# A two-layer gated attention block: the second phase's second MLP product in bf16, split by GpSimd

## What is computed

```python
x = x + tanh(g_ffn[0])   * L0_ffn(layernorm(x))           # fp8 rounding, 256 -> 256
x = x + tanh(g_xattn[1]) * L1_xattn(layernorm(x), ctx)    # q from x, k and v from ctx
h = layernorm(layernorm(x))
y = silu(h @ w1 + fc1_bias)                               # 256 -> 1024
z = y @ w2 + fc2_bias                                     # 1024 -> 256, the second product
x = x + tanh(g_ffn[1]) * (h_residual + 0.5 * z)
```

## Time and profile before

| | us |
|---|---|
| median of 3 runs | 1995.82 (1994.78 to 1996.55) |
| the profiled execution | 1995.66 |
| its span, first to last instruction | 1993.9 |
| TensorE busy | 1727.0 (87%) |
| VectorE busy | 1318.9 (66%) |
| ScalarE busy | 1058.8 (53%) |
| GpSimd busy | 635.6 (32%) |

### The profile page before, as it was taken

One profiled execution on the slowest core, in us unless ns is written; L12 is line 12 of the kernel. 1 busy time (PEld: TensorE's weight loads), 2 busy tenths in 40 slices (PEclk: granted clock), 3 DMA queues, 4 the chain that ended last, 5 costly groups with the idle time before them and its releaser, 6 DMA issues.

```text
span 1993.9 us, 41731 instructions
## 1 busy us (share of the span) xinstructions
PE 1727.0 (87%) x14464; PEld 1336.9 (67%) x14464; DVE 1318.9 (66%) x3182; ACT 1058.8 (53%) x1886; POOL 635.6 (32%) x1236
## 2 busy tenths in 40 slices
PE   3899999999999613679989989899899998998987
PEld 2788888888888512346667666666676666766756
DVE  4677777777777463676676766667767676676532
ACT  3666666666666401445455455554554555545553
POOL 3465665656564312212212122122121221221100
PEclk9999999999999855889999999999999999999999
DMA  5212222121210022433233342342333423323200
GB/s 166 80 54 79 61 71 69 62 77 55 79 46 2 22 97 53 74 65 70 59 74 61 68 73 59 63 68 58 74 59 72 68 58 64 68 58 75 54 12 17
DMA packets 183700, 126.87 MB, mean 64 GB/s; under 512 B 14918, under 2 KB 182860, under 8 KB 183372
## 3 DMA queue, kind: packets, MB, share of 16 engines
q1 hardware_dynamic: 183628, 125.91, 27.3%
HBM read 100.68 MB, written 25.17 MB: 63 GB/s over the span
## 4 chain that ended last, share of the span: by engine, by line
PE 47%; DVE 7%; issue 4%; ACT 2%; SPq 1%; DMA 1%; POOL 1%; DVEq 0%; ACTq 0%; POOLq 0%
PE b_bank L1361 15%; PE b_bank L1441 11%; PE b_bank L1430 6%; DVE b_nm L1263 4%; PE b_scoreT L1408 3%; PE b_bank L1369 3%; PE b_score L1391 2%; PE b_scoreT L1412 2%; ACT b_E L1140 2%; PE b_bank L1520 1%; PE b_bank L1496 1%; DVE b_on L1307 1%; DVE b_st L1221 1%; PE b_bank L1471 1%; DMA b_K<-k_dram 1%
## 5 line engine op out<-in xcount | busy, mean ns | idle before, releaser
L1263 DVE TENSOR_REDUCE b_nm<-b_score 128x4 bf16<-128x1024 f32 x256 | 314.2, 1227 | 147.1 <-PE b_score L1391 147.1
L1140 ACT ACTIVATE b_E<-b_scoreT 128x1024 f32<-128x1024 f32 x256 | 262.0, 1023 | 240.5 <-PE b_scoreT L1412 239.2
L1441 PE MATMUL b_bank<-f,b_Y 128*128 128x256 f32 x1024 | 243.1, 381 | 1.0 <-ACT b_Y L1199 1.0
L31 ACT ACT_TABLE_LOAD x156 | 200.1, 1283 | 63.4 <-PEq L787 50.9
L700 PE MATMUL bank<-W2T,G 128*128 128x256 f32 x1024 | 231.4, 379 | 0.0
L1071 POOL TENSOR_TENSOR b_pool_fence<-b_pool_fence 128x1 f32<-128x1 f32 x96 | 18.8, 195 | 622.3 <-DVE b_mv L1226 622.3
L700 PEld LDWEIGHTS bank<-W2T,G 128*128 128x128 f32 x1024 | 192.0, 190 | 24.9
L1441 PEld LDWEIGHTS b_bank<-f,b_Y 128*128 128x128 f32 x1024 | 185.1, 190 | 23.3 <-ACT b_Y L1199 1.3
L667 PE MATMUL bank<-hT,W1T 128*128 128x256 bf16 x1536 | 178.3, 273 | 7.9 <-DVE hT L593 3.4
L1361 PE MATMUL b_bank<-b_hT,f 128*128 128x256 bf16 x1536 | 175.4, 275 | 2.9 <-DVE b_hT L1286 1.5
L667 PEld LDWEIGHTS bank<-hT,W1T 128*128 128x128 bf16 x1536 | 147.7, 98 | 36.6 <-ACT G L511 15.7
(11 more groups left out here) (215 smaller groups left out, 3452.4 us busy)
## 6 DMA issues: line engine op xcount, KB each, us to landing
b_Q<-q_dram SPq DMA_DIRECT2D x256, 64.0 KB, 3.4
b_K<-k_dram SPq DMA_DIRECT2D x256, 64.0 KB, 3.6
xin<-in_x SPq DMA_DIRECT2D x32, 256.0 KB, 4.8
X<-in_x SPq DMA_DIRECT2D x32, 256.0 KB, 4.6
ctxn<-in_ctx SPq DMA_DIRECT2D x32, 256.0 KB, 2.8
mask_in<-in_mask SPq DMA_DIRECT2D x32, 256.0 KB, 3.1
ctxt<-in_ctxT SPq DMA_DIRECT2D x32, 256.0 KB, 4.5
b_ctxt<-in_ctxT SPq DMA_DIRECT2D x32, 256.0 KB, 2.8
```

The source lines that it names most:

```text
L31: act.add_instruction(mybir.InstLoadActFuncSet(name=nc.get_next_instruction_name(), act_func_set_id=which, ins=[], outs=[]))
L1140: nc.scalar.activation(E[:, pair:pair + 2], scoreT_ps[:, :, :, :], ACT.Exp).then_inc(sig["E"], 1)
L1263: nc.vector.tensor_reduce(pair, score_ps[:, :, :, :], AX.X, ALU.max, negate=True).then_inc(sig["nm"], 1)
L1441: nc.tensor.matmul(bank6[:, t], Y[:, k, tile(t)], f2[:, k], start=k == 0, stop=False)
```

## The change

The second product is made of three bf16 terms. f2 becomes two bf16 halves, high and low, made in the setup by two more VectorE steps. A new tensor YT holds Y's halves. GpSimd makes them in four groups `split(b, j)`, each for two of the eight chunks of Y: a fence, a copy to bf16, a difference. Splits 0 and 1 of a batch stand at the end of its h iteration, behind cT and ahead of the group that ends in b_rh; splits 2 and 3 at the very start of the next one. `product` then makes for each chunk the terms high x high, high x low, low x high: 48 matmuls of 128x128 by 128x256 in bf16 in place of 16 in float32.

The four pieces of the product move from slots 0 to 3 to slots 4, 5, 7 and 8. In exchange the k projection moves from slot 5 to slot 1, with its copy and difference (ScalarE slot 1, VectorE slot 2), and cT is made one iteration earlier, behind b_y. b_res moves from slot 4 to slot 9 of VectorE, the transposes of b_on go to bank 7, and SyncE stores k's spill ahead of q's and the output behind the 16 loads.

```diff
-    f2 = sb("f2", [P, HC, D], F32)
+    f2 = sb("f2", [P, 2, HC, D], BF16)
...
-            step(V_.tensor_tensor(f2[:, :, :], w_2[:, :, :], sc_2[:, :, :], ALU.mult))
+            step(V_.tensor_tensor(w_2[:, :, :], w_2[:, :, :], sc_2[:, :, :], ALU.mult))
+            step(V_.tensor_copy(f2[:, 0], w_2[:, :, :]))
+            step(V_.tensor_tensor(f2[:, 1], w_2[:, :, :], f2[:, 0], ALU.subtract))
...
-            6: [("res", L_OUT, 1, 1), ("klo", L_QKV, 1, 1), ("onlo", L_PROJ, 1, 1), ("Y", L_MLP, 4, 1),
-                ("Y", L_MLP, 4, 4)],
+            6: [("klo", L_QKV, 1, 1), ("res", L_OUT, 1, 1), ("Y", L_MLP, 4, 1), ("Y", L_MLP, 4, 4)],
             7: [("yT", L_FFN, 1, 1), ("ob", L_FFN, 1, 1), ("qlo", L_QKV, 1, 1), ("on", L_PROJ, 2, 2),
-                ("nmT", L_MAX, 1, 1), ("Y", L_MLP, 4, 2)],
+                ("onlo", L_PROJ, 1, 1), ("nmT", L_MAX, 1, 1), ("Y", L_MLP, 4, 2)],
...
@@ GpSimd @@
-                if q:
-                    pool.wait_ge(sig[f"ctxt{q.parity}"], landed(q))
...
+                def split(b, j):
+                    pool.wait_ge(sig["Y"], done(b, per=HC // 2, part=j + 1))
+                    if j == 0:
+                        if (due := done(b, back=1)) is not None:
+                            pool.wait_ge(sig["f2_mm"], due)
                     fence()
+                    nc.gpsimd.tensor_scalar(YT[:, 0, 2 * j:2 * j + 2], Y[:, 2 * j:2 * j + 2], 1.0, 0.0,
+                                            ALU.mult, ALU.add).then_inc(sig["Yhi"], 1)
+                    pool.wait_ge(sig["Yhi"], done(b, per=HC // 2, part=j + 1))
+                    nc.gpsimd.tensor_tensor(YT[:, 1, 2 * j:2 * j + 2], Y[:, 2 * j:2 * j + 2], YT[:, 0, 2 * j:2 * j + 2],
+                                            ALU.subtract).then_inc(sig["Ylo"], 1)
+                if w:
+                    split(w, 2)
+                    split(w, 3)
                 if f:
...
+                if f:
+                    pool.wait_ge(sig[f"ctxt{f.parity}"], landed(f))
...
+                if h:
+                    split(h, 0)
+                    split(h, 1)
                 if o:
                     pool.wait_ge(sig["mv3"], done(o))
...
@@ ScalarE @@
-                        if j == 0:
-                            if (due := done(h, back=1)) is not None:
-                                act.wait_ge(sig["f2_mm"], due)
+                        if (due := done(h, back=1, per=HC // 2, part=j + 1)) is not None:
+                            act.wait_ge(sig["Ylo"], due)
...
@@ TensorE @@
                 def second_product(t, piece):
                     if t == 0 and piece == 0:
-                        free(6, 0)
-                        pe.wait_ge(sig["Y"], done(w, per=HC // 2))
+                        free(6, 1)
+                    if t == 0:
+                        pe.wait_ge(sig["Ylo"], done(w, per=HC // 2, part=2 * piece + 2))
                     half_ = range(HC // 2 * piece, HC // 2 * (piece + 1))
-                    for k in half_:
-                        nc.tensor.matmul(bank6[:, t], Y[:, k, tile(t)], f2[:, k], start=k == 0, stop=False)
+                    product(bank6[:, t], lambda s, k: YT[:, s, k, tile(t)], lambda s, k: f2[:, s, k], half_,
+                            start=piece == 0, stop=False)
...
+                    if slot == 1 and q:
+                        free(6, 0)
+                        pe.wait_ge(sig["ctlo"], done(q))
+                        projection(bank6, 1, 1, cT, "k_mm")
...
-                    if slot < 4 and w:
-                        second_product(slot // 2, slot % 2)
+                    if w:
+                        for i, at in enumerate((4, 5, 7, 8)):
+                            if slot == at:
+                                second_product(i // 2, i % 2)
```

More of the change, by code:

```diff
@@ L1034, in iteration @@
                         sig[f"mask{q.parity}"], 16)
+                    sp.wait_ge(sig["klo"], done(q))
+                    sp.dma_start(k_dram[q.parity].rearrange("s (c p) n -> p (s c) n", p=P),
+                                 ks[:, :, :, :].rearrange("p s c n -> p (s c) n")).then_inc(sig[f"spill{q.parity}"], 16)
                     sp.wait_ge(sig["qlo"], done(q))
@@ L1060, in iteration @@
                                 sig[f"stack{q.parity}"], 16)
+                if w:
+                    sp.wait_ge(sig["res"], done(w))
+                    sp.dma_start(out_d[bass.ds(w.number, 1)].rearrange("o p t d -> p (o t) d"),
+                                 res[:, :, :]).then_inc(sig[f"out{w.parity}"], 16)
             pipeline(sp, iteration, NB, LAGS)
@@ L1150, in iteration @@
                         nc.scalar.activation(xT[:, 0], bank8[:, :, :], ACT.Copy).then_inc(sig["xhi"], 1)
+                    if slot == 1 and q:
+                        act.wait_ge(sig["k_mm"], done(q))
+                        if (due := landed(q, back=1, per=2)) is not None:
+                            act.wait_ge(sig[f"spill{1 - q.parity}"], due)
+                        nc.scalar.activation(ks[:, 0], bank6[:, :, :], ACT.Copy).then_inc(sig["khi"], 1)
                     if slot == 3 and h:
@@ L1160, in iteration @@
                         nc.scalar.activation(qs[:, 0], bank7[:, :, :], ACT.Copy).then_inc(sig["qhi"], 1)
-                    if slot == 5 and q:
-                        act.wait_ge(sig["k_mm"], done(q))
-                        nc.scalar.activation(ks[:, 0], bank6[:, :, :], ACT.Copy).then_inc(sig["khi"], 1)
                     if slot == 10 and o:
@@ L1264, in iteration @@
                                                     negate=True).then_inc(sig["nm"], 1)
+                    if slot == 2 and q:
+                        dve.wait_ge(sig["khi"], done(q))
+                        nc.vector.tensor_tensor(ks[:, 1], bank6[:, :, :], ks[:, 0], ALU.subtract).then_inc(sig["klo"], 1)
                     if slot == 3 and f:
@@ L1292, in iteration @@
                         nc.vector.tensor_tensor(qs[:, 1], bank7[:, :, :], qs[:, 0], ALU.subtract).then_inc(sig["qlo"], 1)
-                    if slot == 6 and q:
-                        dve.wait_ge(sig["khi"], done(q))
-                        nc.vector.tensor_tensor(ks[:, 1], bank6[:, :, :], ks[:, 0], ALU.subtract).then_inc(sig["klo"], 1)
+                    if slot == 9 and w:
+                        dve.wait_ge(sig["f2_mm"], done(w))
+                        dve.wait_ge(sig["base"], done(w))
+                        if (due := landed(w, back=1)) is not None:
+                            dve.wait_ge(sig[f"out{1 - w.parity}"], due)
+                        nc.vector.scalar_tensor_tensor(res[:, :, :], bank6[:, :, :], half_gate[:, 0:1], Xb(w),
+                                                       ALU.mult, ALU.add).then_inc(sig["res"], 1)
                     if slot == 8 and o:
@@ L1311, in iteration @@
                         dve.wait_ge(sig["onhi"], done(o))
[L1312 removed]
+                        nc.vector.tensor_tensor(oT[:, 1], bank7[:, :, :], oT[:, 0], ALU.subtract).then_inc(sig["onlo"], 1)
                 if n:
@@ L1447, in hidden @@
                 def hidden(j):
-                    free(*((6, 3), (7, 5), (8, 3), (6, 4))[j])
+                    free(*((6, 2), (7, 6), (8, 3), (6, 3))[j])
                     if j == 0:
@@ L1508, in iteration @@
                         projection(bank7, 0, 0, xT, "q_mm")
-                    if slot == 5 and q:
-                        free(6, 1)
-                        pe.wait_ge(sig["ctlo"], done(q))
-                        projection(bank6, 1, 1, cT, "k_mm")
                     if slot in (6, 7) and o:
@@ L1522, in iteration @@
                     if slot == 10 and o:
-                        free(6, 2)
+                        free(7, 4)
                         pe.wait_ge(sig["on"], done(o, per=T))
-                        transposed(bank6, on, "onT_mm")
+                        transposed(bank7, on, "onT_mm")
                     if slot == 12 and m:
-                        free(7, 4)
+                        free(7, 5)
                         pe.wait_ge(sig["nm"], done(m, per=NP))
```

30 lines of the change are left out of this document (9 added, 21 removed).

## The result

| us | before | after |
|---|---|---|
| median of the runs | 1995.62 (1994.78 to 1996.55, 4 runs) | 2103.44 (2098.79 to 2105.18, 4 runs) |
| the profiled execution | 1995.66 | 2098.79 |
| its span | 1993.9 | 2097.0 |

The ratio is 1.0537, with a 95% interval from 1.0518 to 1.0555: the changed kernel is slower by 5.4%.

A forecast was written before the change was run, and what follows sets the result against it. The chain to the first maximum b_nm, hidden under the second product, was taken to bound the iteration's start once uncovered: 27 x (1.0 + 2.0) = 81, plus 6.5 for setup and drain, on 1995.66 gives 2083 us, range 2012 to 2125.

The forecast's parts named there:

- The chain: Iteration start: x3, statistics, b_rh, b_hn, first maximum b_nm, run serially under the second product's cover, 0.2 us to spare.
- Up to the second score group: TensorE at the iteration's start: through its remaining work at about 5.3 us instead of 8.5, then waiting for the first maximum.
- D: Time from b_hn's start to b_nm's on VectorE: 1.94 us before, 2.5 forecast, as GpSimd's splits delay the steps.
- a bandwidth shared in parts: Other reading of the VectorE and GpSimd ports: steps stretch only a little, D stays near 1.9 us.
- the formula 34.8 + D: Steady iteration's period in us: second score group at 5.71 + D, then 29.1 of TensorE; 36.2 before.
- the gain: TensorE's saving on the second product per batch: 7.5 us in float32 against 5.5 in bf16, 2.0 us.
- D's break-even: Value of D at which the period equals the 36.2 us of before, rounded to 1.5 us.
- Rival D1: VectorE gets through before GpSimd's copy, D = 1.2, clock holds: 27 x -0.3 + 6.5, 1994 us, no change; chance 6%.
- The clock: The wait ahead of the second score group lowers TensorE's granted clock: 2.0 us per iteration, ends 0 and 2.9.
- rival A: The clock holds despite the wait, each iteration losing only 1.0 us: 2029 us; chance 15%.
- The 27 iterations: Steady iterations with the second product between scores, each 1.0 + 2.0 us longer: 81 us in all.
- The drain: The last batch's four splits in a row ahead of its product: +3 us, between 0 and 6.

The follow-up runs named there:

- e7: The kernel before with the changed kernel's GpSimd program, the splits' results unread, the float32 product at its old place: 2006.62 us, ratio 1.0064.
- e1: The changed kernel with one more GpSimd wait, so that splits 2 and 3 start only after VectorE's b_dn: 2014.51 us, ratio 1.0082.
- e8: The kernel before with the three-term bf16 product at its old place, left operand constant zeros, no splits: 1974.32 us, ratio 0.9904.
- the last kernel above: Changed kernel, splits 2 and 3 behind b_dn, q projection in slot 2; last iterations: product in slots 0 to 3, all splits ahead of b_rh: 1954.48 us.
- both edits: The changed kernel with splits 2 and 3 waiting for b_dn and the q projection moved from slot 4 to slot 2: 1961.08 us, ratio 0.9824.

## Why the prediction was right, point by point

**The bound.** "The chain is hidden with 0.2 us to spare" was the reading from which all else follows, and it holds: the shares of busy time (91% TensorE, 19% GpSimd) spoke for the change, and the change cost 5.4%. The product alone at its old place gave 0.8 of the 1.7 us that it saves there.

**Up to the second score group.** Forecast: b_rh done at 4.4, measured 4.39 (1271.46). TensorE through at 5.3 and a wait of 2.9, measured 5.41 and 3.00. The second group at 5.71 + 2.5 = 8.2, measured 8.41. The wait ahead of the first group I had put on b_E; it is 0.47 on the mask step, b_mb, which has the same length and another owner.

**D.** Forecast 2.5, measured 2.60 and 2.71 in turns, but the parts were dealt otherwise (and my own, 1.2 + 0.4 + 1.0, make 2.6). I had the first b_hn ahead of the copy, the second behind it and b_tg behind the difference. Measured: the first b_hn began 0.03 us after the copy and waited it out, the second waited the difference out, b_tg kept its length, b_up waited 0.3. In e7 it was b_tg and b_dn that paid. The mechanism was right; that the sum came so near is in part luck. Extents of b_hn over the steady stretch, after and then with splits 2 and 3 behind b_dn (shortest, median, longest ns):

```profile
L1269 DVE TENSOR_SCALAR b_hn<-X,b_mv,b_rh x50: 733/1081/1321, 955.4 to 1900.5; 128x256 f32 x44, 128x256 f32<-128x256 f32 x6
```
```profile
L1271 DVE TENSOR_SCALAR b_hn<-X,b_mv,b_rh x50: 405/410/414, 953.3 to 1826.6; 128x256 f32 x44, 128x256 f32<-128x256 f32 x6
```

After, not one of the 50 is short; with GpSimd silent not one is long. The Trainium skill, page "SBUF — State Buffer", section on the two separate sides, has the pair of ports taken for a whole instruction by whoever comes first; these rows agree, and a bandwidth shared in parts (D near 1.9) is out.

**The rest, and the formula 34.8 + D.** Two kernels at the full clock test it: 37.41 with D = 2.61 gives 34.80, and e1's 35.9 of the undisturbed iterations with D = 1.12 gives 34.8. One term of the formula was slightly off: 48 matmuls and two bias rows at 0.114 are 5.7 us, not 5.5, so the gain is 1.8 and not 2.0 (e8 measures 1.73 at the old place); D's break-even, rounded from 1.4 to 1.5, takes off 0.1 the other way. With 5.7 the formula would be 0.2 us over what was measured, so something else in the sum made up for it, by luck. Rival D1 (D = 1.2, clock held, 0.3 us under before) had the right size for what it described, and its condition is one wait on GpSimd away.

**The clock.** Forecast 2.0 us per iteration, measured 1.91. Windows of 4 us around the wait show where:

```profile
1269.00:1273.00 4.00, 3.01 (x34) 1.68 (x31) 2.54 (x6) 2.80 (x5) 3.71 (x9) 1.00 0.12 37
1273.00:1277.00 4.00, 1.52 (x8) 0.85 (x8) 3.85 (x7) 0.55 (x1) 2.36 (x4) 0.78 0.09 30
1277.00:1281.00 4.00, 4.00 (x37) 2.55 (x37) 2.50 (x5) 0.60 (x1) 0.00 (x0) 0.79 0.23 64
1281.00:1285.00 4.00, 4.00 (x47) 2.88 (x46) 2.31 (x8) 1.78 (x3) 0.09 (x1) 1.00 0.00 0
```

It is at 2.4 GHz up to the wait, at 1.2 for a part of the wait and of the work behind it, and back. Over this whole iteration its mean is 0.96, over the next, 0.8 us longer, 0.91. Taking its price from the one iteration of before that had such a wait was what made the forecast, and rival A (2029) wrong. The rows gave 2.5 us; the step down to 2.0, for the part that falls into the wait, was a judgement that came out.

**Where a term was off.** The 27 iterations were 28: the second product starts with the iteration from the second x3. They took 89.4 us, forecast 27 x 3.0 = 81. The drain (from the thirtieth x3 to the end) was sized at +3 and took 10.1. I had counted the four splits of the last batch and not what the place does there: with no scores left, the product was the cover of the b_hn chain too, and the page after shows it gone in each of the last two iterations with a first product (TensorE's timeline: the first of them before, both after, then the last batch):

```profile
1949.59 0.63 PE L1369 MATMUL b_bank<-ident,b_hn 128*128 128x128 f32 x4
```
```profile
2046.64 1.09 PE L1392 MATMUL b_bank<-ident,b_hn 128*128 128x128 f32 x4 [6.53 <-DVE b_tg L1271]
...
2069.59 1.09 PE L1392 MATMUL b_bank<-ident,b_hn 128*128 128x128 f32 x4 [6.53 <-DVE b_tg L1271]
...
2085.21 1.47 PE L1384 MATMUL b_bank<-f,b_YT 128*128 128x256 bf16 x12 [1.14 <-POOL b_YT L1101]
```

Before, the transposes of b_hn wait for nothing. The float32 product at the new place, which has no splits, needs 89.8 us there (from 1960.4 to 2050.2) against 88.1 after, so the place alone makes a loss of this size. It isn't all of it: with the place back, the last kernel above still needs 84.6, with its waits on the splits. The low clock is in it too: the 24 matmuls behind each of the two long waits take 4.04 and 4.50 us, 24 at the full clock 2.78. The setup's two steps took 1.2 + 2.3 = 3.5, as forecast; the first x3 comes 2.6 later. That number is soft: among the kernels above the first x3 stands between 869.6 and 878.4 with the same setup, or all but the same.

In sum 2083 forecast and 2098.8 in the profiled execution; of the 15.6 us between them 8.4 are the iterations, one of them a miscount, 7.1 the drain, 1.0 the one iteration without a second product, less 0.9 of the start.

## What to carry to other kernels

Before work is moved away from a place where the busiest engine seems merely to be working, look at what runs beside it: if a serial chain of other engines ends there with nothing to spare, the work is its cover, and has to be replaced by other work (here the q projection) before it moves. Work given to an idle engine that shares a resource with an engine of that chain belongs where the chain isn't: one wait on GpSimd, 1.3 us long, was worth 89 us, and with both edits the kernel gained as much per iteration as the product saves. When an engine's order is changed for the steady stretch, the first and last iterations have their own covers and queues, and cost here 10 us, of which rows of the steady stretch showed nothing.
